# A graph network with routed experts on one core: edges scheduled in units of 256, two units to a PSUM bank

## What is computed

```python
# x (6250, 256); src, dst (100000,)
h   = segment_sum(ln(x)[dst], src) + ln(x)          # the neighbours' rows, summed by src
x   = x + (h @ gW1 + gb1) @ gW2 + gb2
y   = ln(x)
w   = softmax(y @ Wr + br)                          # one weight for each of 8 experts
for e in range(8):
    a = relu(bn1(y @ W1[e] + b1[e]))
    a = relu(bn2(a @ W2[e] + b2[e]))
    x = x + w[:, e] * (a @ Wo[e] + bo[e])
```

## Time and profile before

| | us |
|---|---|
| runs of the kernel before | 1577.69, 1580.04, 1582.78 |
| their median | 1580.04 |
| the profiled execution: its span | 1595.0 |
| the profiled execution: its own time | not given apart from its span |
| PE busy | 1279.8 |
| DVE busy | 1197.4 |
| ACT busy | 868.3 |
| POOL busy | 805.0 |
| mean granted TensorE clock | 0.928 of 2.4 GHz |

### The profile page before, as it was taken

How to read it: one execution, slowest core, us unless ns; L and a number is a source line. 1 busy time by engine, 2 the same in 40 slices (tenths; PEclk the granted TensorE clock), 3 DMA queues, 4 the chain that set the end, 5 groups by cost and what they waited for, 6 DMA issues and landing times.

```text
span 1595.0 us, 25908 instructions
## 1 busy us (share of the span) xinstructions
PE 1279.8 (80%) x8179; PEld 841.9 (53%) x8179; DVE 1197.4 (75%) x3476; ACT 868.3 (54%) x1623; POOL 805.0 (50%) x864
## 2 busy tenths in 40 slices
PE   3868885557687778888878878898888998788998
PEld 3746652345454445455545545554555666565665
DVE  9999985566667666777777877777778887777865
ACT  7887451344455435454445544555545665555685
POOL 3000006666556666666666666666666556656300
PEclk9969997778799988999999999999999999999999
DMA  9301135333232332333333333343333323332200
GB/s 292 99 0 53 54 100 170 109 98 103 83 103 86 110 91 87 111 88 100 102 89 113 87 90 113 87 116 87 89 111 88 107 83 107 88 105 86 74 11 11
DMA packets 82235, 150.86 MB, mean 95 GB/s; under 512 B 16855, under 2 KB 55034, under 8 KB 82100
## 3 DMA queue, kind: packets, MB, share of 16 engines
q0 software_dynamic: 39840, 108.84, 23.8%
q1 hardware_dynamic: 42260, 40.36, 8.0%
HBM read 129.87 MB, written 19.27 MB: 94 GB/s over the span
## 4 chain that ended last, share of the span: by engine, by line
PE 47%; DVE 24%; issue 12%; another core or an unknown queue 8%; ACT 7%; DVEq 2%; ACTq 0%
PE PA L1555 11%; PE PB L1571 11%; DVE acc L1071 5%; PE PL L1589 4%; DVE zz L837 4%; PE PT L1589 4%; PE PN L1589 3%; DVE zz L838 3%; DVE onehot L1002 2%; DVE xt L1190 2%; ACT PB L742 2%; PE PN L1505 2%; PE PT L1505 1%; PE PT L1504 1%
## 5 line engine op out<-in xcount | busy, mean ns | idle before, releaser
L544 POOL DMA_INDIRECT gbuf<-xn_hilo,dsti x830 | 790.3, 952 | 667.5 <-issue 196.8
L741 ACT ACTIVATE h<-PB,bnt,bns 128x512 f16<-128x512 f32 (+3 forms) x240 | 167.7, 699 | 325.9 <-remote 177.5
L1555 PE MATMUL PA<-yT,wsplit 128*128 128x512 f16 (+3 forms) x1440 | 318.1, 361 | 13.0 <-issue 9.4
L1571 PE MATMUL PB<-h,wsplit 128*128 128x512 f16 (+3 forms) x1440 | 300.3, 347 | 5.6 <-issue 5.6
L730 ACT ACTIVATE h<-PA,bnt,bns 128x512 f16<-128x512 f32 (+3 forms) x240 | 167.8, 699 | 215.8 <-remote 104.2
L1555 PEld LDWEIGHTS PA<-yT,wsplit 128*128 128x128 f16 x1440 | 143.3, 103 | 114.9 <-issue 31.3
L1173 DVE TENSOR_TENSOR h<-PB,h 128x512 f16<-128x512 f32 (+3 forms) x240 | 139.9, 587 | 84.8 <-ACT PB L742 64.5
L1571 PEld LDWEIGHTS PB<-h,wsplit 128*128 128x128 f16 x1440 | 141.2, 101 | 98.3 <-issue 13.0
L1002 DVE TENSOR_SCALAR onehot<-iota_row,srel 128x128 f16<-128x128 f16 x830 | 178.2, 267 | 0.0
L1167 DVE TENSOR_TENSOR h<-PA,h 128x512 f16<-128x512 f32 (+3 forms) x240 | 139.5, 587 | 40.2 <-ACT PA L731 31.8
L1071 DVE TENSOR_TENSOR acc<-acc,PN 128x256 f32 x276 | 114.0, 413 | 71.9 <-issue 23.8
(11 more groups left out here) (250 smaller groups left out, 1856.5 us busy)
## 6 DMA issues: line engine op xcount, KB each, us to landing
gbuf<-xn_hilo,dsti POOLq DMA_INDIRECT x830
xt<-x_whole_bins SPq DMA_DIRECT2D x49, 128.0 KB
out<-xt SPq DMA_DIRECT2D x49, 128.0 KB
acc<-in_x SPq DMA_DIRECT2D x4, 1536.0 KB
x_whole_bins<-acc SPq DMA_DIRECT2D x4, 1536.0 KB, 11.8
xn_hilo<-xt SPq DMA_DIRECT2D x24, 256.0 KB, 2.1
h<-in_L_ffn_W SPq DMA_DIRECT2D x9, 256.0 KB, 4.3
zz<-in_L_ffn_W SPq DMA_DIRECT2D x5, 256.0 KB
```

Of the source, the lines that this page charges most:

```text
L544: pool.indirect_dma_start(gbuf[:, k % SLOTS, :], None, xn_dram, bass.IndirectOffsetOnAxis(dsti[:, k:k + 1], 0)).then_inc(gat[k % SLOTS], 16)
L741: nc.scalar.activation(h2[:, e % 2, 0, h, 0:w], PB[:, h, 0:w], ACT.Relu, bias=sh, scale=sc)
L1555: last = T_.matmul(PA[:, h, 0:w], wsp[0][:, e, k, wp, h * P:(h + 1) * P], yT[:, g % 2, yp, k, 0:w], start=n == 0, stop=n == 5)
L1571: last = T_.matmul(PB[:, h, 0:w], wsp[1][:, e, k, wp, h * P:(h + 1) * P], h1[:, e % 2, yp, k, 0:w], start=n == 0, stop=n == 5)
```

## The change

Edges are scheduled in **units** of 256, not tiles of 128. A unit is gathered as two halves of 128 (two entries), each with its own gather, one-hot matrix and two matmuls, but all four matmuls of a unit add into the same 128 x 256 of PSUM, and DVE adds a unit to acc once. Two units, four entries, share a bank, a signal and a release of slots (a **quad**). There are at most 391 + 48 = 439 units, made up to 440, hence 880 entries for 830, 220 quads for 415 pairs and 440 adds for 830. gbuf and the one-hot matrices have 20 slots for 18 (five quads for nine pairs). The sort stops one step earlier, at runs of 256. The plan is made in quads: 7 ahead of the loop (28 entries for 26). The schedule's table is 440 wide, in one PSUM bank.

```diff
+UNIT = 2 * P
+UNITS = -(-E_EDGES // UNIT)
+BOUND = UNITS + BINS - 1
 EPC = 10
+CHUNKS = -(-BOUND // EPC)
+NU = EPC * CHUNKS
+NQ = NU // 2
+NENT = 2 * NU
-SLOTS = 18
-RING = SLOTS // 2
+SLOTS = 20
+RING = SLOTS // 4
...
+def units_upto(bins):
+    return NU if bins == BINS else need(bins)
+def quads_upto(bins):
+    return -(-units_upto(bins) // 2)
...
-                if k >= SLOTS and k % 2 == 0:
-                    pool.wait_ge(s["ent_done"], k // 2 - RING + 1)
+                if k >= SLOTS and k % 4 == 0:
+                    pool.wait_ge(s["ent_done"], k // 4 - RING + 1)
...
-                for d in range(9, 0 if j < 7 else TILE_LOG, -1):
+                for d in range(9, 0 if j < 7 else UNIT_LOG, -1):
...
-            def onehots(p):
-                for k in (2 * p, 2 * p + 1):
+            def onehots(q):
+                for k in range(4 * q, 4 * q + 4):
                     ins = V.tensor_scalar(onehot[:, k % SLOTS, :], iota_row[:], srel[:, k:k + 1], None, ALU.is_equal)
...
-            def add_pair(p, mask=True):
-                if 2 * p % EPC == 0:
-                    load_bins(2 * p // EPC)
-                dve.wait_ge(s["ent_done"], p + 1)
-                for i in range(2):
-                    k = 2 * p + i
-                    if i and mask and p + RING < NPAIR:
-                        onehots(p + RING)
-                    if k:
-                        dve.wait_ge(s["acc_done"], k)
-                    to = accf[:, bass.ds(regs[0][k % EPC], D)]
-                    V.tensor_tensor(to, to, bank(("E", p))[:, i, :], ALU.add).then_inc(s["acc_done"], 1)
+            def add_quad(q, mask=True):
+                for u in (2 * q, 2 * q + 1):
+                    if u % EPC == 0:
+                        load_bins(u // EPC)
+                    if u == 2 * q:
+                        dve.wait_ge(s["ent_done"], q + 1)
+                    elif mask and q + RING < NQ:
+                        onehots(q + RING)
+                    if u:
+                        dve.wait_ge(s["acc_done"], u)
+                    to = accf[:, bass.ds(regs[0][u % EPC], D)]
+                    V.tensor_tensor(to, to, bank(("E", q))[:, u % 2, :], ALU.add).then_inc(s["acc_done"], 1)
...
-            for i, blk in enumerate([*range(0, NBLK, 2), *range(1, NBLK, 2)]):
+            for i, blk in enumerate([0, 1, 4, 5, 2, 3, 6, 7]):
...
-                for i in range(2):
-                    k = 2 * p + i
+                for k in range(4 * q, 4 * q + 4):
                     m = k % SLOTS
                     pe.wait_ge(gat[m], 16 * (k // SLOTS + 1))
-                    T_.matmul(to[:, i, :], onehot[:, m, :], gbuf[:, m, 0:D], start=True, stop=False)
-                    last = T_.matmul(to[:, i, :], onehot[:, m, :], gbuf[:, m, D:2 * D], start=False, stop=True)
+                    for half in range(2):
+                        last = T_.matmul(to[:, k % 4 // 2, :], onehot[:, m, :], gbuf[:, m, half * D:(half + 1) * D],
+                                         start=k % 2 + half == 0, stop=k % 2 + half == 2)
                 last.then_inc(s["ent_done"], 1)
...
-PRO_PAIRS = 13
+PRO_QUADS = 7
...
-PRO_AT = {"bias": 8, "rows": 8, "shift": 9, "y_T": 10, "y_low": 11}
+PRO_AT = {"bias": 3, "rows": 3, "shift": 4, "y_T": 5, "y_low": 6}
...
-TILE_LOG = 7
+UNIT_LOG = 8
```

More of the change, by code:

```diff
@@ L67, in need, with quads_for @@
     return BOUND * bins // BINS
[L70 to L75, removed]
+def units_upto(bins):
+    return NU if bins == BINS else need(bins)
+def quads_upto(bins):
+    return -(-units_upto(bins) // 2)
+def quads_for(g):
+    return quads_upto(FIRST[g + 1])
 def entry_plan():
-    done = PRO_PAIRS
+    done = PRO_QUADS
     plan = []
@@ L83, in entry_plan @@
         for e in range(EX):
-            goal, left = (pairs_for(g + 1), DUE - e) if e < DUE and g + 1 < G else \
-                (pairs_for(g + 2), EX + DUE - e) if e >= DUE and g + 2 < G else (done, 1)
+            goal, left = (quads_for(g + 1), DUE - e) if e < DUE and g + 1 < G else \
+                (quads_for(g + 2), EX + DUE - e) if e >= DUE and g + 2 < G else (done, 1)
             n = -(-max(goal - done, 0) // left)
@@ L97, in entry_plan @@
             x = EX * (g - 1) + DUE - 1
-            assert sum(len(p) for step in plan[:x] for p in step) + PRO_PAIRS >= pairs_upto(FIRST[g] + 2)
-    assert nhalf(0) == 1 and done == NPAIR and len(flat) == NPAIR - PRO_PAIRS
+            assert sum(len(p) for step in plan[:x] for p in step) + PRO_QUADS >= quads_upto(FIRST[g] + 2)
+    assert nhalf(0) == 1 and done == NQ and len(flat) == NQ - PRO_QUADS
     return plan
@@ L120, in bank_users @@
 def bank_users(plan):
-    users = [("E", p) for p in range(PRO_PAIRS)]
+    users = [("E", p) for p in range(PRO_QUADS)]
     for x, places in enumerate(plan + [[[]] * 5]):
@@ L890, in schedule @@
                 st(V.tensor_scalar(dbc[:], ones[0:BINS, :], sm[:, 9:10], None, ALU.mult), False)
-                st(V.tensor_scalar(Mm[0:BINS, :], iotk[0:BINS, :], sm[:, 6:7], None, ALU.is_ge))
-                st(V.scalar_tensor_tensor(out=Mm[0:BINS, :], in0=iotk[0:BINS, :], scalar=sm[:, 8:9],
+                st(V.tensor_scalar(Mm[0:BINS, :], iotu[0:BINS, :], sm[:, 6:7], None, ALU.is_ge))
+                st(V.scalar_tensor_tensor(out=Mm[0:BINS, :], in0=iotu[0:BINS, :], scalar=sm[:, 8:9],
                                           in1=Mm[0:BINS, :], op0=ALU.is_lt, op1=ALU.mult))
@@ L896, in schedule @@
                 dve.wait_ge(s["sched_pe"], 4)
+                st(V.tensor_tensor(tu, iotu, PA[:, 0, 0:NU], ALU.add), False)
+                st(V.tensor_copy(bk.rearrange("p (u i) -> p u i", i=2),
+                                 PB[:, 0, 0:NU].unsqueeze(2).broadcast_to([P, NU, 2])))
                 for i in range(2):
[L898 to L903, removed]
+                    st(V.tensor_scalar(tk.rearrange("p (u i) -> p u i", i=2)[:, :, i], tu, 2.0, float(i), ALU.mult,
+                                       ALU.add), False)
+                st(V.tensor_scalar(bofs[0:1, :, 0:EPC], bk[0:1, :].rearrange("p (c m i) -> p c m i", m=EPC, i=2)[:, :, :, 0],
+                                   float(D), None, ALU.mult))
                 assert nS[0] == SCHED_T
@@ L1028, in _ @@
                 if blk >= 3:
-                    for p in range(2 * blk - 6, min(2 * blk - 4, RING)):
-                        onehots(p)
+                    onehots(blk - 3)
             dve.wait_ge(s["sched_pe"], 6 + NBLK)
@@ L1203, in _ @@
             dve.wait_ge(s["xnhi_ready"], TWOS)
-            for p in range(PRO_PAIRS):
-                add_pair(p, p >= 4)
-                if p == 3:
+            for p in range(PRO_QUADS):
+                add_quad(p, p >= 2)
+                if p == 1:
                     other_rows()
-                    for q in range(4):
+                    for q in range(2):
                         onehots(RING + q)
@@ L1253, in _ @@
                 for p in plan[x][2]:
-                    add_pair(p)
+                    add_quad(p)
                 lo2(x, 0)
```

63 lines of the change are left out of this document (28 added, 35 removed).

## The result

The changed kernel takes 1665.5 us against 1579.6 us before (four runs of each): **1.053 times as long**, 95% interval 1.051 to 1.055. That is 86 us slower where I forecast 82 us faster; my range ended at 1554. The kernel before took 1582 to 1606 us (medians) on the chips of the later batches, so every experiment is given by its ratio to runs of before on its own chip.

A forecast was written before the change was run, and what follows sets the result against it. It took PE and DVE's coupling through three shared PSUM banks as the loop's limit. Sort and tables 0, prologue 0, loop -83, tail 0 gave 1512 us of span, 1498 us for the runs' median; range 1440 to 1554.

The forecast's parts named there:

- a reserve of 1261/1038, or 21%: Loop, POOL: 830 gathers at 1.25 us need 1038 us but are spread over 1261, so they are not the bound.
- Time goes with the bank writes, some 2 us each.: Loop: PE's writes of PSUM banks set each stage's time; the four-bin stage falls from 249 writes to 170.
- The coupling that I saw at 1004.5 us: Loop: PE, 1.53 us idle, writes bank PN at 1005.50, after DVE read it until 1005.40; three shared banks couple them.
- The stage from 1256 to 1332: Four-bin loop stage with sparse bank writes: PE, busy 71.95 of 76 us, is the bound there; it stays at 76.
- its 5% of loss: Loss beside the bound, 76.00/71.95 = 1.056, applied to all eight loop stages: 1094 us becomes 1155.
- The fours: Loop, POOL: slots released four at a time, not two, still leave POOL sixteen to work on; no cost.
- The slower rival: Loop: each entry's path costs 1.50 to 1.52 us, perhaps by waiting for a one-hot; +77, 1656 us; chance 0.07.
- its share of the chain: Whole kernel: DVE's part of the chain of waits, 24% before, falls under 20%.
- the shorter sort: Before the loop: the sort loses its step at distance 128, all on the path, for -1.3 us.
- The prologue: 236 to 297 us, before the loop: 28 gathers for 26, taken as 0, bounds -15 to +10 us.
- The 32 selection matmuls: Before the loop, on the path: widened from 406 to 430 columns, they add 0.7 us to 11.16.
- The sign of being wrong that I named: Loop: gathers spaced 1.5 us with no wait for PE would show that the slower case holds.

The follow-up runs named there:

- e3: Changed kernel, still 880 gathers, but each unit has its own bank and signal, and releases and one-hots go in twos: 1.037 of before.
- u1: Kernel before with its gathers left out after the first 18, all else kept: 1344.1 us, 0.841 of before.
- e1: Changed kernel with its gathers left out after the first 20, all matmuls, adds and one-hots kept: 1316.0 us, 0.832 of before.
- s2: Kernel before with 20 gather slots for 18, given back to POOL in fours and not in twos: 1.029 of before.
- e2: Changed kernel with DVE's one-hots left out after the first 40 entries, all 880 gathers kept: 1657.7 us, 1.048 of before.
- s3: The kernel of e3 with 50 of its 880 gathers left out, spread evenly, all entries' other work kept: 0.998 of before.
- s1: Kernel before with 20 gather slots and not 18, nothing else changed: 1.002 of before.

## Why the prediction was wrong

- **"So the gathers are not the bound now, with a reserve of 1261/1038, or 21%."** This step failed. POOL's idle time did end with PE's signals, but I read that as PE being late. PE's signals were late, because of the gathers: without them, or with two in 3.29 us, they come in 0.01 us. The reserve assumed that the gathers could run at 1.25 us each while PE's signals release them; the mean was 1.52 us before and 1.51 after. From 830 on each gather added costs 1.25 us of the program (62 us for 50 in e3), with no reserve at all.
- **"Time goes with the bank writes, some 2 us each."** Time went with bank writes before because entries and banks rise together, two to one. Taking 79 of 249 away in the four-bin stage brought nothing, and without gathers the whole change is worth 15 us (u1 and e1), not 83. The coupling that I saw at 1004.5 us is real but small.
- **The stage from 1256 to 1332** was near PE's bound, as I read it (71.95 of 76 us). But it was also the one with the fewest gathers among those of four bins, 48 in 76.1 us by the trace, 1.59 each, and I took its 5% of loss for all stages. After, 55 start in its 92.4 us, and PE is busy for 84.21 of 93 us. No stage with gathers has them below 1.48 us, before or after.
- **The fours** ("so a release in fours still leaves POOL sixteen to work on", no cost): two units to a bank, with one signal and one release, cost 25 to 35 us net. In the kernel before the release alone costs 41 (s2).
- **The slower rival had the right price and the wrong cause.** It said 1.50 to 1.52 us for each entry, +77 us, 1656 (measured +86). Of its cause, a one-hot that holds up each gather by 0.267 us, e2 left nothing. The Trainium skill (SBUF — State Buffer, "Who interferes with whom") has the rule behind that cause; no run here shows it at work, since 840 tensor_scalar instructions fewer changed the median gather by nothing. I gave the rival 0.07 because of its mechanism, though my own rows agreed on its price: a nearly equal price per entry in all stages that have gathers (68/46 = 1.48 to 96/60 = 1.60) should have weighed more than the want of a cause.
- **Right:** DVE's busy time (1050 forecast, 1070 measured), its share of the chain, and the shorter sort in its direction: the first gather is at 233.4 against 235.8, -2.4 for a forecast of -1.3 (such a start differs by 1 to 2 us between traces of like kernels). The prologue, put at 0, gave +1.9 up to the first copy of wT. The 32 selection matmuls took 11.81 us for 11.16, +0.65, forecast +0.7:

```profile
231.69 11.81 PE L1483 MATMUL PT<-h,zz 128*128 128x430 f32 x32
```

- **The sign of being wrong that I named** ("gathers spaced 1.5 us with no wait for PE") came true in half: the mean is 1.51 us, but within a row it is 1.25, and POOL's waits do end with PE's signals, which come late.

Measured against the forecast of -83, the terms are: banks and adds -7 to -15 for -83 (-7 is s3 less s1, with the adds halved and not the banks; -15 is both, without gathers), gathers +52 to +62 for 0, units in fours +25 to +35 for 0, slots +4 or nothing.

## What to carry to other kernels

Where two engines each seem to wait for the other, and the time per item of one stream is the same in every stage, take that stream away in an experiment before pricing anything else: here it was worth 16% of the kernel, and busy shares (50% POOL, 80% PE) gave no hint. A consumer whose input signals come in bursts is not waiting for its producer's work but for the signals, and a timeline shows it, when several engines wake at one moment long after the records that should have woken them. Here a change that halves adds and signals but adds 6% to the gathers was priced mostly by the gathers.

## What was not expected of the hardware

- While indirect gathers follow each other at 1.25 us, TensorE's semaphore signals pass for some 3.5 us, are then mostly held, and come together 2.2 to 3.2 us after the start of the last gather of the row, 1.4 us for each of its gathers after its start, though the gathers' data has landed on time. With 450 gathers in twos, or two in 3.29 us, the delay is 0.01 us. In the kernel before, ACT's and DVE's own signals show no such delay (0.01 us at the 90th percentile of those recorded). What it is that holds them no run here tells.
- A gather of 64 rows of 1024 bytes, or of 128 rows of 512, costs the program what one of 128 rows of 1024 does (1.053 and 1.050 against 1.053).
- The cost shows only above a rate: 450 gathers cost 0.2% of the program, no more than the runs can tell, 665 cost 7%, 880 cost 22%.
